# Two layers on one core: transposes of k and q first in the slot, y gated ahead of N, first weights loaded in the front phase

## The reference, cut to what matters

```python
def step(S, inp):
    qt, kt, vt, gt, bt = inp
    S = S * jnp.exp(gt)[:, None, None]
    kv = jnp.einsum('hk,hkv->hv', kt, S)
    delta = (vt - kv) * bt[:, None]
    S = S + kt[:, :, None] * delta[:, None, :]
    o = jnp.einsum('hk,hkv->hv', qt, S)
    return (S, o)
...
gated = core * jax.nn.silu(z)
gated = gated * jax.lax.rsqrt(jnp.mean(gated * gated, axis=-1, keepdims=True) + EPS)
return (gated * norm_w).reshape(B, Tn, VDIM) @ W_out
```

## Time and profile before

| | |
|---|---|
| median of 3 runs | 3310.9 us (3307.18 to 3311.34) |
| the profiled execution, its own time | 3320.92 us |
| its span in the profile | 3319.2 us |
| mean granted TensorE clock | 0.981 |
| `delta_rule`, first projection to last drain slot | from 312.8 to 2982.9 us of the span |
| PE, DVE, ACT, POOL busy | 3021.5, 2337.6, 1777.8, 1640.1 us |

### The profile page before, as it was taken

The page is one execution under the profiler, slowest core; times in us unless marked ns, Lnnn a source line. Parts: engine busy times, 40 slices in busy tenths (PEclk is TensorE's granted clock), DMA queues, the critical chain, the costliest instruction groups (busy, mean ns, idle before and its releaser), DMA issues. The chain is left out here.

```text
span 3319.2 us, 70198 instructions
## 1 busy us (share of the span) xinstructions
PE 3021.5 (91%) x23017; PEld 2191.0 (66%) x23017; DVE 2337.6 (70%) x4933; ACT 1777.8 (54%) x5786; POOL 1640.1 (49%) x3745
## 2 busy tenths in 40 slices
PE   6997699999999999999999999999999999878998
PEld 4555476766677767766677677766776767765555
DVE  3443577777777777777777777777777777745776
ACT  4222466666666556666666666656666666532332
POOL 1001566666666666666666666666666666620000
PEclk9998899999999999999999999999999999987999
DMA  3000111111111111111111112111111111100000
GB/s 74 0 1 20 37 41 38 38 41 38 40 37 41 35 42 35 41 35 42 35 41 35 43 36 47 38 38 39 44 35 42 38 42 35 35 16 32 7 7 13
DMA packets 447057, 113.77 MB, mean 34 GB/s; under 512 B 350497, under 2 KB 445841, under 8 KB 446673
## 3 DMA queue, kind: packets, MB, share of 16 engines
q1 hardware_dynamic: 446672, 108.98, 14.7%
HBM read 63.85 MB, written 45.09 MB: 33 GB/s over the span
## 5 line engine op out<-in xcount | busy, mean ns | idle before, releaser
L467 POOL TENSOR_TENSOR Tb<-Tb,btmp 64x14 f32<-64x14 f32 (+6 forms) x896 | 314.0, 350 | 70.5
L811 ACT ACTIVATE oq<-bank,gs 128x128 f32<-128x128 f32 x512 | 146.3, 368 | 362.8 <-PE bank L525 362.8
L876 ACT ACTIVATE raw<-bank 128x512 f32<-128x512 f32 x256 | 153.2, 599 | 333.7 <-PE bank L670 325.9
L1134 DVE SCALAR_TENSOR_TENSOR conv<-raw,ckq,conv 128x512 f32<-128x512 f32 x384 | 303.6, 791 | 28.2 <-ACT conv L877 17.1
L1134 DVE SCALAR_TENSOR_TENSOR conv<-raw,cv,conv 128x512 f32<-128x512 f32 x384 | 312.1, 813 | 13.1 <-ACT conv L877 2.0
L463 POOL TENSOR_TENSOR btmp<-Bk,Tb 64x14 f32<-64x14 f32 (+6 forms) x896 | 284.8, 318 | 65.6
L434 POOL TENSOR_TENSOR ty<-ty 128x4 f32<-128x4 f32 x128 | 36.8, 288 | 532.3 <-ACT sq_gat L864 532.3
L1080 DVE SCALAR_TENSOR_TENSOR N<-ET,ty,bank 128x128 f32<-128x128 f32 x512 | 144.2, 342 | 179.5 <-POOL ET L409 178.9
L670 PE MATMUL bank<-xnT,wkq 128*128 128x512 f32 x512 | 253.0, 618 | 13.8 <-DMA ckq<-in_L_attn_conv_w_dram 10.6
L670 PE MATMUL bank<-xnT,wv 128*128 128x512 f32 x512 | 248.9, 609 | 5.2 <-issue 4.7
L739 PE MATMUL bank<-wout_h,gT 128*128 128x256 f32 x1024 | 249.6, 387 | 4.4 <-ACT gT L896 4.4
(11 more groups left out here) (350 smaller groups left out, 7705.1 us busy)
## 6 DMA issues: line engine op xcount, KB each, us to landing
blk_n<-N SPq DMA_DIRECT2D x128, 256.0 KB, 2.9
Tp<-blk_t SPq DMA_DIRECT2D x128, 128.0 KB, 3.0
Wp<-blk_w SPq DMA_DIRECT2D x128, 128.0 KB, 3.1
wkq<-in_L_attn_W_qkvz_dram SPq DMA_DIRECT2D x32, 128.0 KB, 2.5
wv<-in_L_attn_W_qkvz_dram SPq DMA_DIRECT2D x16, 256.0 KB
Bk<-blk_n SPq DMA_DIRECT2D x64, 64.0 KB, 2.8
blk_t<-Tb SPq DMA_DIRECT2D x64, 64.0 KB, 2.5
blk_w<-Wb SPq DMA_DIRECT2D x64, 64.0 KB, 2.5
```

Of the source, the lines that this page charges most:

```text
L467: pool.tensor_tensor(Tb[:, j + 1:, 0:j], Tb[:, j + 1:, 0:j], tmp, ALU.subtract).then_inc(row_rdy, 1)
L811: i = act.activation(oq[:, u, :], bU[7][:, u], ACT.Copy, scale=gs[t.c][:, GAM, u:u + 1])
L876: act.activation(raw[h][:, j, :, 3:], bB[1 - j], ACT.Copy)
L1134: dve.scalar_tensor_tensor(out=conv[h][:, j], in0=raw[h][:, j, :, k:k + 256], scalar=cw[:, j, k:k + 1], in1=conv[h][:, j], op0=ALU.mult, o ...
```

## The change

1. PE: `front` is cut into `front_tp` (the transposes), `decay` and `causal`; `front_tp` goes to the head of the body.
2. ACT: `norms` and `silu` go ahead of `from_state`.
3. DVE: `silu` goes from behind `strict` to behind `xev16`.
4. The first head's weights and taps (`wkq`, `ckq`, `wv`, `cv`) are allocated outside and loaded at the end of the queue of `front`; `weights` skips them. The two blocks in memory are cleared from `S` in four DMAs in place of two from `conv[0]`, whose clear (line 351) is gone.
5. The products with `wqkT` leave `second_layer` and run in the drain, one chunk of both sequences per slot, with one more drain slot; ACT copies them to `qk`.

```diff
@@ delta_rule @@
-                sp.dma_start(units(td, 0, 2 * U), conv[0][:].rearrange("p j b n -> p (j b) n").rearrange(
-                    "p a (c n) -> p (a c) n", n=P)).then_inc(tz_in, 16)
-                sp.dma_start(units(wd, 0, 2 * U), conv[0][:].rearrange("p j b n -> p (j b) n").rearrange(
-                    "p a (c n) -> p (a c) n", n=P)).then_inc(tz_in, 16)
+                for half in range(2):
+                    sp.dma_start(units(td, half * U, U), S[:]).then_inc(tz_in, 16)
+                    sp.dma_start(units(wd, half * U, U), S[:]).then_inc(tz_in, 16)
...
+                    first = t.i is None and t.off < C
-                    if t.c == 0:
+                    if t.c == 0 and not first:
...
-                    if t.c == 1:
+                    if t.c == 1 and not first:
...
-                pool.memset(conv[0][:], 0.0).then_inc(setup, 1)
-                pool.memset(S[:], 0.0)
+                pool.memset(S[:], 0.0).then_inc(setup, 1)
...
-                def front(s):
+                def front_tp(s):
...
+                def decay(s):
...
+                def causal(s):
...
+                def low_rank(s):
+                    c = last_chunk(s, S_E + 4)
+                    if c is None or c >= C:
+                        return
+                    pe.wait_ge(ln_out, c + 1)
+                    pe.wait_ge(attn_rdy, STEPS)
+                    pe.wait_ge(N_rdy, STEPS)
+                    if c:
+                        pe.wait_ge(qk_out, c)
+                    for h in range(2):
+                        n = 2 * c + h
+                        for k in range(KT):
+                            i = pe.matmul(bank[3][:, 32 * h:32 * h + 32], xnT[:, k, n * P:(n + 1) * P], l2["wqkT"][:, k, :],
+                                          start=(k == 0), stop=(k == KT - 1))
+                    i.then_inc(qk_mm, 1)
                 def body(s):
+                    front_tp(s)
                     state_in(s)
                     x64(s)
                     x16(s)
-                    front(s)
+                    decay(s)
+                    causal(s)
...
                     zproj(s)
+                    low_rank(s)
                     project_out(s)
...
+                def low_rank_ev(s):
+                    c = last_chunk(s, S_E + 4)
+                    if c is None or c >= C:
+                        return
+                    act.wait_ge(qk_mm, c + 1)
+                    act.activation(l2["qk"][:, 2 * c:2 * c + 2, :].rearrange("p n d -> p (n d)"), bank[3][:, 0:64],
+                                   ACT.Copy).then_inc(qk_out, 1)
                 def body(s):
                     ztanh(s)
+                    norms(s)
+                    silu(s)
                     from_state(s)
                     xev64(s)
-                    norms(s)
                     expo(s)
-                    silu(s)
...
                     gtev(s)
+                    low_rank_ev(s)
                     norm_ev(s)
...
                     xev16(s)
+                    silu(s)
                     add_w64(s)
                     add_w1(s)
                     strict(s)
-                    silu(s)
@@ front @@
+                sp.dma_start(hd["wkq"][:, :, 0:P], wq[:, :, 0, P:2 * P]).then_inc(hd["wkq_in"], 16)
+                sp.dma_start(hd["wkq"][:, :, P:], wq[:, :, 0, 0:P]).then_inc(hd["wkq_in"], 16)
+                sp.dma_start(hd["ckq"][:, 0:1, :], cw[:, HK:HK + 1, :]).then_inc(hd["wkq_in"], 16)
+                sp.dma_start(hd["ckq"][:, 1:2, :], cw[:, 0:1, :]).then_inc(hd["wkq_in"], 16)
+                sp.dma_start(hd["wv"][:], wq[:, :, 0, 2 * P:4 * P]).then_inc(hd["wv_in"], 16)
+                sp.dma_start(hd["cv"][:], cw[:, 2 * HK:2 * HK + 2, :]).then_inc(hd["wv_in"], 16)
@@ second_layer @@
-                    for n in range(NT):
-                        for c in range(KT):
-                            i = pe.matmul(psq[:, n, :], xnT[:, c, n * P:(n + 1) * P], wqkT[:, c, :], start=(c == 0), stop=(c == KT - 1))
-                    i.then_inc(pe_s, 1)
...
-                    v.wait_ge(pe_s, 1)
-                    v.tensor_reduce(mx[:], psq[:, :, 0:DQ], AX.X, ALU.max)
+                    v.tensor_reduce(mx[:], qk[:, :, 0:DQ], AX.X, ALU.max)
```

More of the change, by code:

```diff
@@ L106, in masks, with delta_rule @@
     return m
-def delta_rule(nc, ins, m, acc, xn, xnT, gates):
+def delta_rule(nc, ins, m, l2, hd, acc, xn, xnT, gates):
     S_P, S_S, S_F, S_L, S_D, S_E = 0, 1, 2, 5, 6, 7
@@ L119, in delta_rule @@
         ev = ctx.enter_context(phase_semaphores(nc))
-        wkq = sb("wkq", [P, KT, 256])
-        wv = sb("wv", [P, KT, 256])
+        wkq, wv, ckq, cv, wkq_in, wv_in = (hd[k] for k in ("wkq", "wv", "ckq", "cv", "wkq_in", "wv_in"))
         wz = sb("wz_h", [P, KT, 256])
         wout = sb("wout_h", [P, 2, D])
-        ckq = sb("ckq", [P, 2, 4])
-        cv = sb("cv", [P, 2, 4])
         nw = sb("nw", [P, 1])
@@ L184, in blocks @@
             return bass.AP(tensor=d.tensor, offset=0, ap=[[16 * (P + 1), 64], [P, 16], [1, 16]])
-        (setup, wkq_in, wv_in, wz_in, wo_in, nw_in, tz_in, n_out, blk_in, t_out, t_in, w_out, w_in) = (ev(n) for n in (
-            "setup", "wkq_in", "wv_in", "wz_in", "wo_in", "nw_in", "tz_in", "n_out", "blk_in", "t_out", "t_in", "w_out",
+        (setup, wz_in, wo_in, nw_in, tz_in, n_out, blk_in, t_out, t_in, w_out, w_in) = (ev(n) for n in (
+            "setup", "wz_in", "wo_in", "nw_in", "tz_in", "n_out", "blk_in", "t_out", "t_in", "w_out",
             "w_in"))
@@ L208, in delta_rule @@
             "st", "mv", "ve", "rs", "xn", "tp", "out"))
+        qk_mm, qk_out = ev("ln1_qk_mm"), ev("ln1_qk_out")
         lst = sb("ln1_stats", [P, NT, 6])
@@ L220, in pipeline @@
                     body(Slot(i, k))
-            for n in range(STEPS, STEPS + 10):
+            for n in range(STEPS, STEPS + 11):
                 body(Slot(None, n))
@@ L306, in base_out @@
                     wait(sp, t_in, before)
-                    sp.wait_ge(tz_in, 32)
+                    sp.wait_ge(tz_in, 64)
                     sp.dma_start(blocks(td), Tb[:]).then_inc(t_out, 16)
@@ L626, in front @@
                     i.then_inc(kq_tp, 1)
+                def decay(s):
+                    t = s.back(S_F)
+                    if not t.live:
+                        return
                     pe.wait_ge(gtri_rdy, t.done())
@@ L631, in front @@
                               stop=True).then_inc(dt_mm, 1)
+                def causal(s):
+                    t = s.back(S_F)
+                    if not t.live:
+                        return
+                    y = kq_of(t)
                     wait(pe, N_rdy, t.done(1))
@@ L1175, in routed_tiles, with front @@
     }
-def front(nc, ins, m, l2, r, x, xn, xnT):
+def front(nc, ins, m, l2, r, hd, x, xn, xnT):
     xnS = r["xnS"]
@@ L1817, in second_layer @@
         wide_in = sem("wide_in")
-        wqkT, wT, gw, leb, gtb, midb = (l2[k] for k in ("wqkT", "wT", "gw", "leb", "gtb", "midb"))
+        qk, wT, gw, leb, gtb, midb = (l2[k] for k in ("qk", "wT", "gw", "leb", "gtb", "midb"))
         pk = sb("pk", [P, NT, 96])
@@ L2281, in build @@
             "wT": {k: sb("wT_" + k, [P, KT, D]) for k in ("Wog", "Wig", "Wo")},
+            "qk": sb("l1_qk", [P, NT, 32]),
             "gw": sb("gw", [P, D]),
@@ L2288, in build @@
             gates = c2.enter_context(nc.sbuf_tensor("gates", [P, STEPS, NKIND, U], F32))
+            hd = {k: c2.enter_context(nc.sbuf_tensor(k, sh, F32)) for k, sh in (
+                ("wkq", [P, KT, 256]), ("wv", [P, KT, 256]), ("ckq", [P, 2, 4]), ("cv", [P, 2, 4]))}
+            hd["wkq_in"], hd["wv_in"] = nc.alloc_semaphore("wkq_in"), nc.alloc_semaphore("wv_in")
             with ExitStack() as c3:
                 r = routed_tiles(nc, c3)
-                front(nc, ins, m, l2, r, x, xn, xnT)
+                front(nc, ins, m, l2, r, hd, x, xn, xnT)
                 routed_loop(nc, ins, m, r, x, xn, xnT, gates)
-            delta_rule(nc, ins, m, x, xn, xnT, gates)
+            delta_rule(nc, ins, m, l2, hd, x, xn, xnT, gates)
         second_layer(nc, ins, m, l2, x, xn, xnT, out)
```

13 lines of the change are left out of this document (8 added, 5 removed).

## The result

Changed kernel: median 3194.87 us (3191.85 to 3206.27, 4 runs) against 3311.12 us (3307.18 to 3313.1, 4 runs) before; ratio 0.9657, 95% interval 0.9631 to 0.9682. It is 116.3 us faster; 3193 us was forecast. Its profiled execution took 3206.27 us, with a span of 3204.4.

A forecast was written before the change was run, and what follows sets the result against it. TensorE's work and a GpSimd-DMA chain to the odd x16 were taken as the bound. Loop 102, start 5.1, fill 2 and end 8.3 sum to 117.4: 3203.5 us profiled, 3193 us median, range 3140 to 3242.

The forecast's parts named there:

- The bound: Loop: TensorE's own work plus a chain through GpSimd and DMA to the odd slot's x16 (first matmul on `Tp`).
- The new pair: Two loop slots, from one kd product's start to the next but one: 38.87 us, a gain of 1.70 per pair.
- The loop term: Gain over all 60 pairs of slots in the steady loop: 60 x 1.70 = 102 us.
- their own price is nil in the even slot: Moving TensorE's transposes to the slot's head costs nothing in even slots; in odd slots 0.49 us leaves the stretch behind x16.
- I take 0: ScalarE's squares and tanh ahead of the state's copy: later `oq` and `Xs64` cost nothing, as their readers come late.
- the 1.11 us of the odd `Us`: Odd slot: gating y ahead of N removes the `Us` wait; x16 to next kd product falls from 9.01 to 7.41 us.
- The gate's collision with GpSimd: The moved gate delays GpSimd's row 5 and norms by some 1.1 us; the later 1.06 us loss goes, sum unchanged.
- Start and fill, 5.1 + 2: First projection 5.1 us sooner, bound by GpSimd's setup; shorter v wait in the fill gains 2 us.
- End, 8.3: 64 matmul instructions leave the second layer's head and return in the drain as eight groups of 8: 8.3 us gained.
- Gapless TensorE: Rival: the chain shortens and TensorE runs without gaps; pair 37.5 us, 198 us gained, 3113 us; chance 0.12.
- One unreturned gate: Rival: the gate costs GpSimd 1.1 us on the norms and returns none; pair 40.0, 3262 us; chance 0.15.
- the slower case: Rival: two GpSimd stalls of about 1.1 us per pair; 15 us slower, 3326 us; chance 0.06.

The follow-up runs named there:

- the last series: Five runs each: changed kernel 3202.61 us; changed kernel with the 64 products back at the second layer's head 3206.21; kernel before with three loop orders, old ends 3212.39.
- the exchange on GpSimd: Changed kernel with rows 1 to 5 of the block inverse put ahead of GpSimd's output scales: 3120.46 us, ratio 0.9411; changed kernel beside it 3190.21 us.

## Why the prediction was right

**The bound.** Right that the pair turns on GpSimd, and shown from both sides: 0.60 us more on GpSimd's rows made the pair 0.57 longer, eight more transposes on TensorE in the even slot nothing, and scales out of the rows' way made it 1.2 shorter. Two readings in it were off. The DMA is not the only last link: the way through mask, N, `Us` and A' is only 0.4 us shorter. And the even norms did not wait for row 5 "whatever ScalarE did sooner": in the mean row 5 ended 0.21 us ahead of them, and they waited for the squares. The large wait for `yv` and the gain it seemed to promise (132.5 us by the waits) were no guide; x16 of the odd slot moved only from A+31.57 to A+31.28.

**The new pair.** 38.87 forecast, 38.76 measured (38.69 and 38.86 in the two further profiles of the changed kernel). x16 to A'' is 7.48 in the mean, where 7.24 to 7.41 was forecast, and the chain 0.28 shorter than the 31.56 kept. With TensorE's and ScalarE's orders alone it is 0.25 shorter, and there the even norms begin 0.26 us sooner, since the squares are done 3 us earlier. The loop term was 102; the first profile has 108.7, the others 112.6 and 102.5.

**TensorE's order, "their own price is nil in the even slot".** Wrong taken alone: 0.5 us in the even slot, through `oq` and the squares; ScalarE's new order took that away.

**ScalarE's order, "I take 0".** This term was put at nothing, and it is the step that failed. It is not free either way: alone +2.33 us per pair, with TensorE's order it is the whole gain (-1.87 together, +0.26 the one alone). I had seen that N would not stand behind the norms, but put it under the gate.

**The gate's place, the 1.11 us of the odd `Us`.** Wrong as the cause: alone it gives 0.50 per pair, and on top of the two others nothing (38.78 against 38.69). The sum of the three singles is +0.26 - 0.50 + 2.33 = +2.09 per pair, and together they give -1.79. The forecast's 9.01 - 0.49 - 1.11 arrived at the right length because u then ends last, whatever freed `Us`. That this sum came out right is luck: neither of its two terms does alone what it was credited with.

**The gate's collision with GpSimd.** Right in place and kind. Rows 1 to 5, from their start to their end, went from 4.96 to 5.79 us in the mean: +0.82, a little under the 1.1 forecast; from the mask's end to the last row went from 7.93 to 6.86, -1.07. Where the gate came later it took the time from norms and mask instead (from norms to mask 2.97 us with VectorE's order alone, 2.81 with eight transposes more, 2.02 before). By the rule of the Trainium skill's page "SBUF — State Buffer", section "SBUF: two separate sides", GpSimd is locked out for the whole of a VectorE instruction with two SBUF inputs. The trace agrees: the row operation that meets the gate starts 0.13 us behind it and ends 0.14 us behind it (1.23 us in place of 0.28, the gate 1.22). That the odd slot's gate meets only "norms and mask that are not on the chain" did not hold with VectorE's order alone, where it put N 0.95 us back.

**Start and fill, 5.1 + 2.** The first projection came 4.3 sooner here and 5.5 and 5.9 in the two further profiles: 5.1 was right. The fill's 2 was wrong in sign. Its v wait went, but the fill took 91.1, 90.3 and 90.4 us against 88.8, at granted clocks of 0.77, 0.76 and 0.76 against 0.82; net 2.0, 3.9 and 4.4 for the 7.1 forecast. The clock is 0.78 with the three orders and the old start too, in a fill of 89.2 us, so the new start is not what brought it down. What does, and what lengthens the fill by another 1.1 to 1.9 us with the new start, was not tried.

**End, 8.3.** Measured 5.2, 8.8 and 5.4 against the one profile before: near where three of the four last groups ran at 2.4 GHz, 3 too much where all ran at 1.2. Against the three profiles with the old end in the last series (37.8, 40.4 and 41.0) the third is 3.5, 6.1 and 6.7, so the term is not known better than that. I had taken the clock of a stretch with hardly a TensorE wait in it.

**The rivals.** "Gapless TensorE" had the right price for the wrong kernel: pair 37.5 and 3113 us; the exchange on GpSimd gave 37.47 and 3120. One unreturned gate, and the slower case, did not come, since the lost time at row 5 came back at rows 6 and on.

So the total hit (117.4 forecast, 114.8 in the spans) rests on a loop term 6.7 too small and two end terms 5.1 and 3.1 too large, with 1.1 more lost in the drain's first part and the second layer. That these errors cancel is luck, and the number itself moves: the gain by the medians was 116.3, 126.8 and 121.4 us in the three series (ratios 0.9657, 0.9626 and 0.963).

## What to carry to other kernels

Find the chain that a pair or a group of slots turns on, and ask of each engine on it what stands in its queue ahead of the chain's work and could stand behind it: two lines exchanged on GpSimd gave 70 us more, where TensorE's waits named VectorE's `Us` and a DMA, 52 us together. Orders of several engines are not additive: two of these three lose time alone and the third gives a quarter of the gain, so price them as one path (transposes, squares, norms, mask, N) and test the pairs, not only the single parts. Price what a clock can change at both of its levels.

## What was not expected of the hardware

In the second layer VectorE's copy of `qk` took 1.15 us while GpSimd cleared a tile (1.38 us, at the same time); from PSUM before, with no such clear beside it, the same copy took 0.41 (the row is of the changed kernel; the other five profiles with the new end have 1.15 too):

```profile
2882.85 1.15 DVE L1928 COPY a_k<-l_qk 128x256 f32<-128x256 f32 x1
```

It has one input, and was not tried apart. The other: the same program had the drain's products at one clock level or the other from one profile to the next, worth some 3.5 us of the 8.3 that this part of the change was to bring.
